# Cross-attention and expert FFN on one core: eight passes (four head groups by two query halves) in place of four, V kept once with nine columns a head, a spare PSUM bank, and another tail

## What is computed

```
x: (1, 1024, 128)   ctx: (1, 6404, 96)   16 heads of 8 channels
q = layernorm(x) @ Wq + bq;  k = ctx @ Wk + bk;  v = ctx @ Wv + bv
att = softmax(clip(q k^T * 8**-0.5)) v          # per head: 1024 queries x 6404 keys
x = x + att @ Wo + bo
n = layernorm(x)
main = gelu(n @ W1m + b1m) @ W2m + b2m           # 128 -> 512 -> 128
top-2 of 8 experts by softmax(mean(n) @ w_gate + b_gate); same shape of FFN for each
x = x + a * main + (1 - a) * sum of the two weighted experts
```

## Time and profile before

| what | value |
|---|---|
| median of 3 runs | 855.53 us (854.18 to 856.58) |
| the profiled execution, its own time | 855.05 us |
| its span, first to last instruction | 853.3 us |
| ACT busy | 775.5 us (91%) |
| PE busy / PEld busy | 751.9 us (88%) / 241.4 us (28%) |
| DVE busy / POOL busy | 80.0 us (9%) / 21.8 us (3%) |
| mean granted TensorE clock | 0.987 of full speed |

### The profile page before, as it was taken

The page is one execution under the profiler, slowest core; times in us unless marked ns, Lnnn a source line. Parts: engine busy times, 40 slices in busy tenths (PEclk is TensorE's granted clock), DMA queues, the critical chain, the costliest instruction groups (busy, mean ns, idle before and its releaser), DMA issues.

```text
span 853.3 us, 12912 instructions
## 1 busy us (share of the span) xinstructions
PE 751.9 (88%) x5352; PEld 241.4 (28%) x5352; DVE 80.0 (9%) x231; ACT 775.5 (91%) x636; POOL 21.8 (3%) x35
## 2 busy tenths in 40 slices
PE   3989888888898888888988888888988899888798
PEld 2652222222222222222222222222222223222467
DVE  6631220000010000000100000000100001000300
ACT  2769999999999999999999999999999999999450
POOL 9000000000000000000000000000000000000000
PEclk9999999999999999999999999999999999999799
DMA  5234441300011000011100011000000000000010
GB/s 176 82 103 121 118 130 25 81 16 16 17 41 28 20 17 17 16 24 24 36 21 16 17 22 26 16 17 16 17 1 1 2 1 1 1 1 1 3 50 25
DMA packets 20713, 29.04 MB, mean 34 GB/s; under 512 B 7830, under 2 KB 11276, under 8 KB 20652
## 3 DMA queue, kind: packets, MB, share of 16 engines
q1 hardware_dynamic: 19628, 27.40, 12.7%
q0 software_dynamic: 480, 0.66, 0.3%
q10 hardware_dynamic: 544, 0.12, 0.1%
HBM read 20.02 MB, written 8.13 MB: 33 GB/s over the span
## 4 chain that ended last, share of the span: by engine, by line
PE 42%; ACT 33%; issue 22%; DVE 1%; DMA 1%; SPq 0%; ACTq 0%
ACT region_ctxT L430 33%; PE po L913 19%; PE ps L894 12%; PE ps L995 3%; PE po L1007 3%; PE po L795 1%; PE ps L784 1%; DVE xn L514 1%; PE po L916 1%; DMA region_ctx<-in_ctx 1%; PE ps L772 1%; PE po L1010 0%; PE ps L896 0%; PE po L814 0%; PE ps L856 0%
## 5 line engine op out<-in xcount | busy, mean ns | idle before, releaser
L430 ACT ACTIVATE region_ctxT<-ps 128x1536 f32<-128x1536 f32 x536 | 723.0, 1675 | 8.6 <-PE ps L894 8.1
L913 PE MATMUL po<-region_ctxT,region_v 128*32 128x512 f32 x3200 | 427.0, 606 | 0.2 <-ACT region_ctxT L430 0.2
L894 PE MATMUL ps<-qst,region_k 32*128 32x512 f32 x1600 | 268.9, 493 | 76.1 <-ACT region_ctxT L430 75.9
L894 PEld LDWEIGHTS ps<-qst,region_k 32*128 32x128 f32 x1600 | 104.3, 181 | 445.8 <-ACT region_ctxT L430 436.9
L913 PEld LDWEIGHTS po<-region_ctxT,region_v 128*32 128x32 f32 x3200 | 63.0, 108 | 100.2 <-issue 97.3
L623 DVE COPY region_v<-vall 128x160 f32<-128x160 f32 x40 | 12.6, 318 | 405.8 <-PE po L913 402.5
L285 ACT ACTIVATE region_ctxT<-ps 96x512 f32<-96x512 f32 (+1 forms) x13 | 7.6, 582 | 13.5 <-PE ps L772 13.5
L772 PE MATMUL ps<-ident,region_ctx 128*96 128x128 f32 x50 | 9.4, 324 | 6.7 <-DMA region_ctx<-in_ctx 6.7
L658 DVE COPY region_kT<-po 128x512 f32<-128x512 f32 x2 | 1.4, 692 | 145.3 <-PE po L916 82.5
L784 PE MATMUL ps<-region_ctxT,wk_sb 96*128 96x512 f32 (+1 forms) x26 | 14.4, 652 | 0.0
L298 ACT ACTIVATE vall<-po 128x512 f32<-128x512 f32 (+1 forms) x13 | 7.5, 585 | 7.1 <-PE po L795 7.1
(11 more groups left out here) (163 smaller groups left out, 204.6 us busy)
## 6 DMA issues: line engine op xcount, KB each, us to landing
region_k<-k_dram SPq DMA_DIRECT2D x320, 40.0 KB, 1.9
k_dram<-kparts SPq DMA_DIRECT2D x18, 320.0 KB, 3.4
qst<-q_dram SPq DMA_DIRECT2D x64, 32.0 KB
region_ctx<-in_ctx SPq DMA_DIRECT2D x2, 624.0 KB, 8.5
q_dram<-region_k SPq DMA_DIRECT2D x2, 512.0 KB, 4.1
k_dram<-kparts SPq DMA_DIRECT2D x2, 322.0 KB, 3.3
region_ctx<-in_ctx SPq DMA_DIRECT2D x1, 576.0 KB, 6.8
xres<-in_x SPq DMA_DIRECT2D x1, 512.0 KB, 4.3
```

Source lines behind the costliest of these rows:

```text
L430: act.activation(probs[:, t % NPR, :], ps[slot_of_tile(t) % NSB][:, :], ACT.Exp, scale=SCALE).then_inc(exp_ready, 1)
L894: last = mm(dst, kst[r, kt * P:(kt + 1) * P], qst[r, g % 2, queries], start=True, stop=True)
L913: last = mm(po[half][QUAD * j:QUAD * (j + 1), :], vst[:, kt, QUAD * j:QUAD * (j + 1)], src, start=first, stop=last_one, skip_group_check=True)
```

## The change

The four groups over both query halves become eight passes: for query half 0 the four head groups, then for half 1 the four head groups. Each pass has 201 chunks (67 tiles), so there are again 536 tiles, but the keys are gone through eight times and K is loaded eight times, not four. Pass p adds up in the bank `po[p % 2]`; the other bank is spare, and takes the transposes of the finished pass (`spare_job`), which no longer take a score buffer. V is stored once for all heads, `v9` with 8 channels and a one for each head; the value product's stationary operand has 9 columns at the same four column groups of 32, and DVE's refills go. All four groups' q stay on chip (`load_q` after segments 2, 3 and 4 of pass 0). The exp has a scale of 4 ln 2 (its inverse is in q) and a bias read from a column `ebias`. After pass 3, the first half's projection, layer norm, transposes and the first main layer run inside the loop in the spare bank. In the tail, half 0's GELU is one instruction of 128x2048 without a pointer; the square roots and the gate's exp become powers on POOL; the FFN's biases enter by one product and two adds instead of eight products; hidden tiles use four banks, not six; and the output leaves in three pieces. `D_PLAN`, a list of steps that DVE could take over, is empty, so nothing of that code runs.

The core of the diff:

```diff
+QSCALE = SCALE / (4.0 * math.log(2.0))
+ESCALE = 4.0 * math.log(2.0)
+V9 = D + 1
+NORM_GAP = 2
+EPI_AT = [2, 4, 8, 10, 11, 12, 13]
+OUT_TILES = [(0, QT // 2), (QT // 2, 3 * QT // 4), (3 * QT // 4, QT)]
+PASSES = [(g, half) for half in range(NHALF) for g in range(NG)]
+D_PLAN = [
+]
+def pv_bank(p):
+    return p % 2
@@ sync
-                    if s == 2:
-                        load_q(sp, 1)
+                    if 2 <= s < 1 + NG:
+                        load_q(sp, s - 1)
                 load_k_tail(sp)
+                for p in range(1, NP):
+                    for s in range(NSEG):
+                        sp.wait_ge(scores_ready, tile_of_segment(p - 1, s) + 1)
+                        load_k(sp, p, s)
@@ gpsimd
-            pool.memset(region_v[:, :], 0.0).then_inc(vones_ready, 1)
+            pool.memset(v9[:, :, :, D:V9], 1.0).then_inc(vones_ready, 1)
+            pool.memset(vtail[:, :, :], 0.0).then_inc(vones_ready, 1)
+                pool.tensor_tensor(rstd[:, 3, r], rstd[:, 0, r], powers[:, 0:QT // 2], ALU.pow).then_inc(std_ready, 1)
+            pool.wait_ge(msum_ready, 2)
+            pool.tensor_tensor(gate[0:1, 2, :], euler[:, :], gate[0:1, 1, :], ALU.pow).then_inc(exp_gate, 1)
@@ scalar
-                    act.activation(probs[:, t % NPR, :], ps[slot_of_tile(t) % NSB][:, :], ACT.Exp, scale=SCALE).then_inc(exp_ready, 1)
+                    act.activation(probs[:, t % NPR, :], ps[t % NSB][:, :], ACT.Exp, bias=ebias[:, 0:1],
+                                   scale=ESCALE).then_inc(exp_ready, 1)
+            act.activation(hid[0][:, :, 0:BANK], pre[:, :, :], ACT.Gelu_apprx_tanh).then_inc(main0_ready, 1)
@@ tensor
+                def spare_job(n):
+                    ...
+                        pe.wait_ge(o_taken, i + 1)
+                        dst = po[1 - pv_bank(i + 1)]
+                        for a in range(QT // 2):
+                            last = tr(dst[:, a * P:(a + 1) * P], oraw[:, i % 2, a * P:(a + 1) * P], ident[:, :])
+                pe.wait_ge(v_done, VCH)
+                for t in range(NT):
+                    score_tile(t + NSB)
+                    spare_job(n)
+                    att_transpose(0, po[EPI_BANK])
+                    project_out(0, po[EPI_BANK])
+                    xn_transpose(0, po[EPI_BANK])
+                    first_main(EPI_AT.index(t - epilogue) - 3)
+                    pe.wait_ge(exp_ready, t + 1)
+                    values_step(n)
+            second_layer(0, 0)
+            xn_transpose(1, bank(4))
```

More of the change, by code:

```diff
@@ L83 @@
[L83 to L98, removed]
+MIX_BANK = 5
+NORM_GAP = 2
+EPI_AT = [2, 4, 8, 10, 11, 12, 13]
+D_GAP = 6
+EPI_BANK = 1
+OUT_TILES = [(0, QT // 2), (QT // 2, 3 * QT // 4), (3 * QT // 4, QT)]
+ALPHA_COL = C + (E + 1) * CB
@@ new lines @@
+assert FULL % NSEG == 0
+MAGIC = 1.5 * 2.0 ** 21 + 0.25 * 383
+C5 = 1.3595107320097566
+R0 = 0.7929909
+A1, B1 = 0.17040694762516811, 1.272584845263978
+A2, B2 = -1.1993498695574036, 0.7288907538224542
+PASSES = [(g, half) for half in range(NHALF) for g in range(NG)]
+NP = len(PASSES)
+LAST_OF_HALF = [max(p for p, (_, h) in enumerate(PASSES) if h == half) for half in range(NHALF)]
+D_PLAN = [
+]
+DKT = [[kt for p, kt, _, _ in D_PLAN if p == q] for q in range(NP)]
+STEPS = [(p, kt) for p in range(NP) for kt in range(FULL + 1) if kt not in DKT[p]]
@@ new lines, in values_through, with tile_of_segment, spare_of_segment @@
+def values_through(t):
+    last = max(CHUNKS[CPT * t + m][0] for m in range(CPT))
+    return max(n for n, (_, kind, i) in enumerate(VALUES) if kind == 0 and i == last) + 1
+def tile_of_segment(p, s):
+    return max(c for c, (n, _) in enumerate(CHUNKS)
+               if STEPS[n][0] == p and (STEPS[n][1] < FULL and STEPS[n][1] // SEG_T == s)) // CPT
+def spare_of_segment(p, s):
+    return max([SPARE_OF["score", GH * d + GH - 1] + 1 for d, (q, kt, _, _) in enumerate(D_PLAN)
+                if q == p and kt // SEG_T == s], default=0)
@@ L101, in seg_cols, with pass_at @@
+def pass_at(t):
+    return min(p for p in range(NP) if t <= PASS_END[p])
+def pv_bank(p):
+    return p % 2
 def seg_cols(s):
@@ new lines, in xn_transpose, with first_main @@
+            def xn_transpose(n, dst):
+                pe.wait_ge(xn_ready, QT + (n + 1) * QT // 2)
+                for i, t in enumerate(range(n * QT // 2, (n + 1) * QT // 2)):
+                    last = tr(dst[:, i * P:(i + 1) * P], xn[:, t, :], ident[:, :])
+                last.then_inc(xnT_psum, 1)
+            def first_main(cb):
+                if cb == 0:
+                    pe.wait_ge(xnT_ready, NHALF + 1)
+                else:
+                    pe.wait_ge(pre_taken, cb)
+                mm(po[EPI_BANK][:, :], w1m_sb[:, cb * P:(cb + 1) * P], xnT[:, 0:BANK], start=True, stop=True).then_inc(pre_psum, 1)
@@ L950, in _ @@
+                pe.wait_ge(o_taken, NP)
+                for a in range(QT // 2):
+                    last = tr(bank(0)[:, a * P:(a + 1) * P], oraw[:, (NP - 1) % 2, a * P:(a + 1) * P], ident[:, :])
+                last.then_inc(tok_psum, 1)
             with pe.Else():
@@ L1013, in second_layer @@
+                    if e == TOPK and any(t == t1 - 1 for _, t1 in OUT_TILES):
+                        last.then_inc(ffn_psum, 1)
                 if e < TOPK and half == 1:
                     last.then_inc(ffn2_done, 1)
[L1017 to L1020 removed]
+            second_layer(0, 0)
+            xn_transpose(1, bank(4))
+            pe.wait_ge(xnT_ready, 2 * NHALF)
+            first_layer(0, range(CB, CB + 1))
```

527 lines of the change are left out of this document (295 added, 232 removed).

## The result

The kernel after takes 903.91 us (median of 4 runs, 902.54 to 905.43) against 855.31 us for the kernel before beside it (854.18 to 856.58): a ratio of 1.0568, 95% interval 1.0545 to 1.0591. Its profiled execution has a span of 901.9 us against 853.3, with a mean granted clock of 0.979 against 0.987. The prediction was 902.7.

A forecast was written before the change was run, and what follows sets the result against it. ACT's exp, 536 times, was taken to bound the kernel. Terms -5.5 + 0.9 - 1.0 + 48.2 + 10.3 - 2.5 - 3.2 = +47.2 us gave a median of 902.7 us, range 891 to 911.

The forecast's parts named there:

- Item 3: Start: PE waits for V's last copy before the first score, so the first exp comes 0.9 us later.
- Item 4: Prologue: a smaller clearing on POOL frees DVE earlier, 4.5 us, plus 1.0 for less half clock: -5.5 us.
- item 5: Ends of passes: seven ends and the half's epilogue lose 7.9 us against 10.5 before: -2.5 us.
- Item 1: Exp's bias column: 0.09 us more for each of 536 exps, pitch 1.432 us: +48.2 us.
- Item 2: K's arrival in pass 0: stalls at tiles 26, 33 and 67, behind q batches: +10.3 us.
- item 7: Tail: eight bias products go (-3.3 us), with smaller terms both ways: -3.2 us in all.
- A: Rival: the column is free, pitch stays 1.342, K's stalls grow: +8.2, 863.8 us; chance 0.08.
- B: Rival: K is in time and the stalls do not come: 892.4 us; chance 0.07.
- C: Rival: PE becomes the bound, nine columns keeping heads from running side by side: about 1060 us; chance 0.02.
- item 6: V of nine columns: value products stay at 1.06 us for four heads; the end of DVE's refills gives nothing.
- D: Rival: POOL's powers are slow or half clock follows each stall, 5 to 10 us more: 908 to 913; chance 0.06.
- The 1.0: Term of -1.0 us before tile 67: ACT's idle 1.02 at 63.01 would lie in the shadow.

The follow-up runs named there:

- e2: The kernel before with only the exp's bias read from a column of zeros: 897.22 us, ratio 1.0493.
- e3: The kernel after with head groups 2 and 3's q loaded after the K loads of passes 1 and 2: 893.38 us, ratio 1.0448.
- e4: The kernel after with the exp's bias a constant again and the late q loads: 857.86 us, ratio 1.0036.
- e5: The kernel after with constant bias, late q loads, and each next segment's store issued ahead of the loads in pass 0: 850.98 us, ratio 0.995.
- e10: e7 with the epilogue spread over more tiles and the first two score tiles ahead of PE's wait for V's last copies: 844.32 us, ratio 0.9868.
- e7: e5 with POOL waiting for x's eight scaled tiles before its ten transfers and its clearing of V's ninth columns: 845.97 us, ratio 0.9887.
- e6: The kernel before with POOL waiting until DVE has scaled x's eight tiles before it clears `region_v`: 846.74 us, ratio 0.9902.
- e8: e5 with the first half's epilogue pieces on tiles 2, 6, 11, 16, 20, 24, 28: 849.31 us, ratio 0.9929.
- e11: e10 with POOL's wait behind its ten transfers, ahead of its clearing of V's ninth columns only: 843.63 us, ratio 0.9864.

## Why the prediction was right, step by step

The time was right (902.7 against 903.91), and so were the two mechanisms that carry it; smaller terms were off and nearly cancelled: +1.9 (items 3 and 4) + 3.7 (item 5) - 0.9 (items 1 and 2) - 3.3 (item 7) is +1.4, and the profiled sum was off by +1.4 (48.6 against 47.2). That 9.8 us of deviations leave 1.4 is luck. Of the rivals, A falls with the pitch, B with the waits ahead of tiles 26 and 33, C with item 6, and D with powers of 1.0 us; half clock did follow the stall at the change of pass.

*Item 1, the column, right.* The pitch went from 1.344 to 1.431, in `e2` to 1.432; with 0.0875, between the two, 0.0875 x 536 = 46.9 against 48.2. L411 against L285 at 512 columns gave the price at 1536. The Trainium skill ("ScalarE: Activation LUTs", What ACT_TABLE_LOAD costs) states some 93 ns for a pointer operand; the traces here have 87 to 88.

*Item 2, K's arrival, right in place and size.* Waits at tiles 26 and 33 and at the change of pass; from first exp to tile 67 the growth is 15.6 where 6.0 + 10.3 - 1.0 = 15.3 was forecast; less 67 x 0.0875 = 5.9 for the pitch it is 9.7, against 9.3. (The 1.0 did not fall into the shadow: ACT still waits 0.68 and 0.34 ahead of tiles 4 and 5.) `e3` takes 8.8 of it away. The cause was named too narrowly: SP's standing still for each store is as large a part, which shows once the exps are faster (`e4`, `e5`).

*Item 3, start, right:* 0.66 between copy and exp, where 0.75 was reckoned, and `e10` takes it away.

*Item 4, prologue, too large a gain.* I forecast -5.5; the last copy of V came 3.4 earlier. The step that failed is "DVE is then free at about 15.9": the hold ended at 17.1. The clearing of 128x816 took 1.61 us, not 0.8 (816 single columns, nine apart, against 6400 in a row in 5.45), and the hold again began ahead of it. Nor did the 1.0 come that I added for less half clock: the granted clock was 0.50 from 16 to 22 us, as it had been from 20 to 25. By the Trainium skill ("Advanced Engine Details and Errata", Mode Summary), on which the prediction drew, the hold should end with the second of POOL's two memsets; it did (16.97, and PE's wait ends at 17.11). The rest, 3.7, was still to be had, as `e7` shows.

*Item 5, ends of passes, wrong in sign.* Forecast -2.5, measured 42.2 - 469 x 0.0875 = +1.2. Seven ends at 0.7 was right for six (67 tiles in 96.63, of which the pitch makes 95.9). The first end cost 2.7, with the half clock behind the stall, which I had let end at tile 67. The epilogue cost 4.1, not 3. Timeline of ACT there:

```profile
460.94 11.56 ACT L477 ACTIVATE region_ctxT<-ps,ebias 128x1536 f32<-128x1536 f32 x8 [0.43 <-PE ps L998]
473.35 3.03 ACT L477 ACTIVATE region_ctxT<-ps,ebias 128x1536 f32<-128x1536 f32 x2 [0.85 <-PE ps L998]
477.79 1.54 ACT L477 ACTIVATE region_ctxT<-ps,ebias 128x1536 f32<-128x1536 f32 x1 [1.41 <-PE ps L998]
480.24 20.15 ACT L477 ACTIVATE region_ctxT<-ps,ebias 128x1536 f32<-128x1536 f32 x14 [0.91 <-PE ps L998]
```

The waits of 0.85 to 1.41 stand behind the first-layer products (timeline of PE):

```profile
470.77 1.13 PE L977 MATMUL po<-xnT,w1m_sb 128*128 128x512 f32 x2
471.82 1.05 PE L1058 MATMUL po<-region_ctxT,v 128*9 128x512 f32 x8
...
475.21 1.12 PE L977 MATMUL po<-xnT,w1m_sb 128*128 128x512 f32 x2 [0.42 <-DVE region_ctx L655]
```

One keeps PE for 1.05 us (470.77 to 471.82), more than the 0.86 I had, and they stand in neighbouring tiles. The third stood another 0.42 us, until DVE had copied the one before out of the spare bank, which all four use. I had also let the lead of 0.4 us count once for all; it is used up by the first piece. The layer norm's power on POOL took 1.04 us, and PE had no wait at the transposes behind it.

*Item 6, nine columns, right:* L913's 427.0 us busy became L1058's 424.7.

*Item 7, tail, too small a gain.* Forecast -3.2, measured -6.5. From the start of the experts' layers on it is -4.7 (36.3 to 31.6), where -2.6 was forecast: the mis-sized term is "0.41 each: -3.3"; the eight products cost 0.6 each, 4.9, and the half clock, of which 0.5 was counted, did not come. Ahead of them it is -1.7 (30.2 to 28.5 us after the last exp), where -0.6 was forecast, and that is the clock's doing: the granted clock there was 0.50 for 10.2 us in the profile before and for 6.8 in the one after. PE's first layer, in the kernel before and, with the same tail but only 3.4 us of half clock, in `e6`:

```profile
797.81 6.45 PE L995 MATMUL ps<-xnT,w1m_sb 128*128 128x512 f32 x8 [0.78 <-ACT xnT L446]
```

```profile
789.36 3.70 PE L996 MATMUL ps<-xnT,w1m_sb 128*128 128x512 f32 x8 [0.78 <-ACT xnT L447]
```

`e6` has its experts' layers start 26.9 us after the last exp; the new tail, in `e8` with 3.4 us of half clock as well, takes 27.8, and PE stands 2.60 of them for the experts' loads. So at equal clock the way became some 0.9 longer, not 0.6 shorter, and the whole tail's gain is 4.7 - 0.9 = 3.8, an estimate from these four profiles; the rest of the 6.5 is luck with the clock. POOL's powers were as assumed, 1.04 and 1.01 us; the gate's took 1.63.

## What to carry to other kernels

Where one engine paces a loop of hundreds of instructions, price every operand of that instruction first: an operand that cancels out of the result cost 42.8 us here, more than all the rest of the change was worth. Halving a loop's pass halves the time in which its operands must arrive, and the queue that brings them should issue the next store before it waits for the last. And look at the prologue of the kernel as it stands: one wait on POOL gave 8.5 us to the kernel before, and the whole new structure, mended, only some 3 more (843.63 against 846.74).

## What the hardware showed that I had not expected

A clearing queued on POOL holds DVE's scaling from SBUF to SBUF from some 2 us ahead of the clearing's own recorded start (12.68 against 14.90 in the kernel before). The hold is gone when POOL waits for DVE on a semaphore first (eight scalings in 2.1 us in `e6` and `e11`, against 9.4); the transfers that POOL issues do not hold them.

Half clock after PE's idle time is not decided by the length of the idle time in this range. PE stood 2.93 us ahead of the first expert's layer in the kernel after and ran it at full clock (7.13 us); it stood 2.75 in `e11` and ran at full clock; it stood 2.82 in `e10` and took 9.98 us. That is these two lines, of `e11` and of `e10`:

```profile
810.24 7.13 PE L1137 MATMUL ps<-xnT,region_ctx 128*128 128x512 f32 x16 [2.75 <-DMA b2rows<-in_b2e]
```

```profile
809.90 9.98 PE L1137 MATMUL ps<-xnT,region_ctx 128*128 128x512 f32 x16 [2.82 <-DMA b2rows<-in_b2e]
```

In `e10` the stretch from 810 to 814 us has a granted clock of 0.50, 1.2 GHz, in `e11` 1.00, 2.4 GHz. Of the eleven runs that have this stand, of 2.60 to 2.93 us, five ran the layer in 7.13 us, five in 8.83 and one in 9.98; the shortest stand, 2.60 in `e8`, is among the slow ones, 2.61 in `e7` among the fast. So 1.7 to 2.9 us of a profile's tail can come or not come without a cause in the kernel that these traces show.
